# Joining the expert block and the final sum of a small language-model tower, with the last two groups' results kept on chip

## What is computed

```
merged = einsum('bked,bke->bed', tok, vals)          # 32 sequences x 32 experts x 256
h1 = gelu(einsum('bei,eih->beh', [merged, 1], w1))    # w1: 32 experts, 257 x 1024
o  = einsum('bej,ejo->beo', [h1, 1], w2)              # w2: 32 experts, 1025 x 256
out = zeros_like(x).at[b, idx].add(o * vals)          # each expert's row back to its 8 tokens
h = h + out
```

## Time and profile before

| what | value |
|---|---|
| median of 3 runs | 860.26 us (857.64 to 861.04) |
| the profiled execution's own time | 861.66 us |
| its span, first to last instruction | 859.9 us |
| mean TensorE clock granted | 0.937 |
| PE, DVE, POOL, ACT busy | 82%, 70%, 52%, 41% of the span |
| DMA of the experts' weights | 32 transfers of 2 MB |

### The profile page before, as it was taken

How to read it: one execution, slowest core, us unless ns; L and a number is a source line. 1 busy time by engine, 2 the same in 40 slices (tenths; PEclk the granted TensorE clock), 3 DMA queues, 4 the chain that set the end, 5 groups by cost and what they waited for, 6 DMA issues and landing times. The chain is left out here.

```text
span 859.9 us, 20461 instructions
## 1 busy us (share of the span) xinstructions
PE 701.9 (82%) x7740; PEld 479.6 (56%) x7740; DVE 600.9 (70%) x853; ACT 353.4 (41%) x563; POOL 447.4 (52%) x250
## 2 busy tenths in 40 slices
PE   6577679868999999999999999994899859766674
PEld 4466444436777777777777777763677524322232
DVE  3688548888999999999999999992577621000014
ACT  3366534434544455544554454542555321210000
POOL 1788400004999999999999999992122100000000
PEclk9699979997999999999999999996999969988895
DMA  4100000000001010000000000002920199999977
GB/s 113 50 2 0 0 0 0 0 0 16 14 11 37 14 37 12 10 8 12 12 12 10 9 12 12 15 15 66 401 87 2 30 367 409 413 414 421 413 313 251
DMA packets 47291, 86.34 MB, mean 100 GB/s; under 512 B 5552, under 2 KB 30704, under 8 KB 47120
## 3 DMA queue, kind: packets, MB, share of 16 engines
q1 hardware_dynamic: 43696, 83.33, 26.2%
q10 hardware_dynamic: 3552, 2.43, 0.9%
HBM read 76.31 MB, written 9.44 MB: 100 GB/s over the span
## 5 line engine op out<-in xcount | busy, mean ns | idle before, releaser
L907 POOL TENSOR_TENSOR read<-state,q_pos 128x1024 f32<-128x1024 f32 x128 | 300.3, 2365 | 28.5 <-DVE state L1016 22.4
L1016 DVE TENSOR_TENSOR_SCAN state<-fac,ps_up 128x1024 f32<-128x1024 f32 x128 | 289.9, 2277 | 8.6 <-ACT fac L951 8.6
L951 ACT ACTIVATE fac<-ps_xf 128x1016 f32<-128x1016 f32 x128 | 130.2, 1017 | 176.4 <-PE ps_xf L1050 162.8
L1050 PEld LDWEIGHTS ps_xf<-hot,xtab 64*128 64x128 f32 x2048 | 126.3, 189 | 58.0 <-ACT fac L951 43.4
L1050 PE MATMUL ps_xf<-hot,xtab 64*128 64x128 f32 x2048 | 149.2, 285 | 11.0 <-ACT fac L951 8.9
L1050 PE MATMUL ps_up<-hot,utab 64*128 64x128 f32 x2048 | 140.7, 277 | 18.3 <-DVE state L1016 18.3
L1050 PEld LDWEIGHTS ps_up<-hot,utab 64*128 64x128 f32 x2048 | 127.0, 190 | 23.8 <-issue 17.7
L916 POOL TENSOR_TENSOR utab<-tab 128x1024 f32 (+1 forms) x32 | 64.7, 2022 | 95.5 <-SPq L85 95.5
L1095 PE MATMUL ps_o<-read,sel 128*32 128x256 f32 x1024 | 82.7, 395 | 3.7 <-POOL read L907 3.7
L1669 DVE COPY h_t<-ps_ht 128x512 f32<-128x512 f32 x16 | 10.3, 686 | 86.1 <-PE ps_ht L1700 86.0
L1684 PE MATMUL ps<-w_sb,mq 128*32 128x512 f32 x256 | 38.4, 739 | 27.7 <-DMA w_sb<-in_L_ffn_w 22.6
(11 more groups left out here) (200 smaller groups left out, 953.4 us busy)
## 6 DMA issues: line engine op xcount, KB each, us to landing
w_sb<-in_L_ffn_w SPq DMA_DIRECT2D x32, 2048.0 KB, 19.2
rec_out<-osb SPq DMA_DIRECT2D x128, 32.0 KB, 1.5
ao<-rec_out SPq DMA_DIRECT2D x8, 512.0 KB, 4.1
out_dram<-h SPq DMA_DIRECT2D x8, 256.0 KB, 2.5
out_dram<-h ACTq DMA_DIRECT2D x8, 256.0 KB, 3.1
tok<-in_x SPq DMA_DIRECT2D x2, 512.0 KB, 8.1
exp_out<-eo SPq DMA_DIRECT2D x8, 128.0 KB, 18.6
oq<-exp_out SPq DMA_DIRECT2D x8, 128.0 KB, 3.0
```

Of the source, the lines that this page charges most:

```text
L907: nc.gpsimd.tensor_tensor(read[n % 2][:], state[n % 4][:].rearrange("p (b i t) -> p b i t", b=2, i=IB), q_pos[x.s][:, :, x.k].unsqueeze(2) ...
L951: nc.scalar.activation(fac[n % 2][:].rearrange("p (n t) -> p n t", t=T)[:, :, 1:], ps_x[:].rearrange("p (n t) -> p n t", t=T)[:, :, 1:], A ...
L1016: nc.vector.tensor_tensor_scan(state[n % 4][:], fac[n % 2][:], ps_u[n % 2][:], 0.0, ALU.mult, ALU.add)\
L1050: last = nc.tensor.matmul(dst[:, b * 512 + col * T:b * 512 + (col + 1) * T], stationary[rows], pos[rows], start=True, stop=True)
```

## The change

`experts` and `combine` become one block with its loops written out.

- PE reads `merged` directly; `mq` and its copies go. ACT loads the Gelu table before the first group.
- Only the results of groups 0 to 5 (24 experts, `STORED`) are stored. When ACT has seen the stores of both `eo` buffers land, ACT (no longer SP) reloads them into `oq` with four transfers of 24 rows by 8 KB.
- Group 6: DVE builds a 0/1 matrix `spread` in the place of `merged`, and PE permutes `eo[:, 0]` with eight matmuls (`spread_rows`) into the four PSUM banks that held `ps_1`. DVE adds that to `oq`, once the reload has landed.
- Group 7: `rows_of_last` permutes `eo[:, 1]` by rows with four matmuls, DVE copies them to `last_rows`, and a second set of four matmuls per quad (`output_last`) adds them, with `last_picks`. `last_picks` is made by 32 matmuls (`picks_of_last`) between the first layers of groups 0 and 1.
- The final sum's matmuls, additions and stores follow in the same block, each quad with eight matmuls in place of four.

The core of the diff, with the programs of ACT, SP, DVE and PE in this order:

```diff
+STORED = X - 2 * QB
...
-            def operands(i, s):
-                q = 2 * i + s
-                act.wait_ge(l2[s], START + 2 * i)
-                nc.scalar.copy(mq[s][:], merged[:, :, bass.ds(QB * q, QB)]).then_inc(mq_ok, 1)
...
+        sel_ok, h1_mm, gl, ht, htok, eo_ok = (sem(n) for n in ("sel_ok", "h1_mm", "gl", "ht", "htok", "eo_ok"))
...
+            for g in range(GROUPS):
+                hidden(g)
+                if g + 2 < GROUPS:
+                    selections(g + 2)
+            for s in range(2):
+                act.wait_ge(eo_st[s], START + 16 * (GROUPS // 2 - 1))
+            src = exp_out.rearrange("x (q j) e -> j x q e", j=QB)
+            for j in range(QB):
+                act.dma_start(oq[j * X:j * X + STORED], src[j, 0:STORED]).then_inc(f_ld, 16)
+            store_rows(act, 1)
...
-            for s in range(2):
-                store(TURNS - 1, s)
-            for s in range(2):
-                sp.wait_ge(eo_st[s], START + 16 * TURNS)
-            for h in range(2):
-                reload(h)
+            first_weights(2)
+            for g in range(2, GROUPS):
+                if g + 1 < GROUPS:
+                    first_weights(g + 1)
+                second_weights(g)
+                store(g - 2)
+            store_rows(sp, 0)
...
+            for g in range(GROUPS):
+                for h in range(2):
+                    hidden(g, h)
+                if g == GROUPS - 1:
+                    dve.wait_ge(row_mm, SPREAD_MM)
+                    dve.wait_ge(f_ld, START + 16 * QB)
+                    nc.vector.tensor_tensor(oq[:], oq[:], ps_s, ALU.add).then_inc(row_ok, 1)
+                results(g)
+                if g == GROUPS - 2:
+                    dve.wait_ge(h1_mm, START + GROUPS)
+                    nc.vector.tensor_tensor(spread, at_row[:].unsqueeze(2).broadcast_to([P, B, X]),
+                                            at_expert[:].unsqueeze(1).broadcast_to([P, B, X]), ALU.mult)\
+                        .then_inc(row_ok, 1)
+            dve.wait_ge(row_mm, ROWS_MM)
+            nc.vector.tensor_copy(last_rows[:], ps_p).then_inc(row_ok, 1)
+            for q in range(QUADS):
+                dve.wait_ge(f_mm, START + q + 1)
+                rows = h2[:, QB * q:QB * (q + 1)]
+                nc.vector.tensor_tensor(rows, ps_q[q % 2][:, :, 0:E], rows, ALU.add).then_inc(f_add, 1)
...
+            def first_layer(g):
+                s = g % 2
+                pe.wait_ge(gl, START + g - 1)
...
+            def picks_of_last():
+                pe.wait_ge(row_ok, STRIP)
+                for q in range(QUADS):
+                    at = QUADS - 1 - q
+                    for j in range(QB):
+                        rows = slice(j * X, (j + 1) * X)
+                        last = nc.tensor.matmul(ps_t[rows, q], strip[rows, at:at + X], picked[rows, q],
+                                                start=True, stop=True)
+                last.then_inc(row_mm, 1)
+            def spread_rows():
+                pe.wait_ge(row_ok, SPREAD)
+                pe.wait_ge(gl, START + GROUPS)
+                for q in range(QUADS):
+                    last = nc.tensor.matmul(ps_s[:, q], spread[:, QB * q:QB * (q + 1)].rearrange("p j x -> p (j x)"),
+                                            eo[:, 0], start=True, stop=True)
+                last.then_inc(row_mm, 1)
+            def rows_of_last():
+                pe.wait_ge(eo_ok, START + GROUPS)
+                for j in range(QB):
+                    last = nc.tensor.matmul(ps_p[j * X:(j + 1) * X],
+                                            ident[:].rearrange("p (n j) -> p j n", j=QB)[:, j],
+                                            eo[:, 1], start=True, stop=True)
+                last.then_inc(row_mm, 1)
+            def output_stored(q):
+                if q > 1:
+                    pe.wait_ge(f_add, START + q - 1)
+                for j in range(QB):
+                    rows = slice(j * X, (j + 1) * X)
+                    nc.tensor.matmul(ps_q[q % 2][:, j, 0:E], picked[rows, q], oq[rows, q], start=True, stop=False)
+            def output_last(q):
+                for j in range(QB):
+                    rows = slice(j * X, (j + 1) * X)
+                    last = nc.tensor.matmul(ps_q[q % 2][:, j, 0:E], last_picks[rows, q], last_rows[rows],
+                                            start=False, stop=True)
+                last.then_inc(f_mm, 1)
...
+            first_layer(0)
+            picks_of_last()
+            first_layer(1)
...
+            transpose_hidden(GROUPS - 1)
+            second_bias(GROUPS - 1)
+            spread_rows()
+            second_layer(GROUPS - 1, 0)
+            pe.wait_ge(row_ok, SUMS)
+            output_stored(0)
+            second_layer(GROUPS - 1, 1)
+            rows_of_last()
+            pe.wait_ge(row_ok, ROWS)
+            output_last(0)
+            for q in range(1, QUADS):
+                output_stored(q)
+                output_last(q)
```

More of the change, by code:

```diff
@@ L1567, in load_w2, with experts @@
         .then_inc(done[h], 16)
-def experts(nc, a, m, sem, sb):
-    ident, merged, exp_out, oq = m["ident"], m["merged"], m["exp_out"], m["oq"]
+def experts(nc, a, m, sem, sb, out):
+    ident, merged, exp_out, h2, picked = m["ident"], m["merged"], m["exp_out"], m["h2"], m["picked"]
     w1, w2, b1, b2, w1_ld, w2_ld = m["w1_sb"], m["w2_sb"], m["b1_sb"], m["b2_sb"], m["w1_ld"], m["w2_ld"]
-    mq = [sb(f"mq{s}", [P, KT, QB, B]) for s in range(2)]
     sel = [sb(f"sel{s}", [X, QB, B]) for s in range(2)]
@@ L1578, in experts @@
     eo = sb("eo", [P, 2, E])
[L1580 to L1589 removed]
+    oq = sb("oq", [P, QUADS, E])
@@ L1607, in _, with selections @@
-            operands(0, 0)
-            operands(0, 1)
-            with nc.scalar.Fori(0, TURNS - 1) as i:
-                for s in range(2):
-                    hidden(i, s)
-                    operands(i + 1, s)
-            for s in range(2):
-                hidden(TURNS - 1, s)
+            def selections(g):
+                if g > 1:
+                    act.wait_ge(l2[g % 2], START + 2 * (g // 2))
+                nc.scalar.copy(sel[g % 2][:], ident[0:X, QB * g:QB * (g + 1)].unsqueeze(2)
+                               .broadcast_to([X, QB, B])).then_inc(sel_ok, 1)
@@ L1618, in _ @@
             m["start"](sp)
[L1620 to L1632, removed]
@@ L1640, in second_weights @@
+            def second_weights(g):
                 for h in range(2):
[L1641 to L1651, removed]
@@ L1661, in _ @@
+            store_rows(sp, 0)
         @block.vector
         def _(dve):
[L1663 to L1669, removed]
-                    dve.wait_ge(l2[s], START + 2 * i + 2)
-                    dve.wait_ge(eo_st[s], START + 16 * i)
-                    nc.vector.tensor_copy(eo[:, s], ps_2[s][:, 0:E]).then_inc(eo_ok, 1)
+            ch = m["vch"]
@@ L1683, in first_layer @@
                         for j in range(QB):
-                            last = nc.tensor.matmul(ps_1[s][j * B:(j + 1) * B, cols], mq[s][:, k, j],
+                            last = nc.tensor.matmul(ps_1[s][j * B:(j + 1) * B, cols], merged[:, k, QB * g + j],
                                                     w1[s][:, j, k, cols], start=k == 0, stop=False,
@@ L1765, in _ @@
+            def output_stored(q):
+                if q > 1:
+                    pe.wait_ge(f_add, START + q - 1)
                 for j in range(QB):
                     rows = slice(j * X, (j + 1) * X)
-                    last = nc.tensor.matmul(ps[q % 2][:, j, 0:E], picked[rows, q], oq[rows, q], start=True, stop=True)
-                last.then_inc(f_mm, 1)
-        @block.vector
-        def _(dve):
-            for q in range(QUADS):
-                dve.wait_ge(f_mm, START + q + 1)
-                rows = h2[:, QB * q:QB * (q + 1)]
-                nc.vector.tensor_tensor(rows, ps[q % 2][:, :, 0:E], rows, ALU.add).then_inc(f_add, 1)
+                    nc.tensor.matmul(ps_q[q % 2][:, j, 0:E], picked[rows, q], oq[rows, q], start=True, stop=False)
@@ new lines, in _ @@
+            for g in range(GROUPS - 1):
+                transpose_hidden(g)
+                second_bias(g)
+                for h in range(2):
+                    second_layer(g, h)
+                if g + 2 < GROUPS:
+                    first_layer(g + 2)
+            transpose_hidden(GROUPS - 1)
[5 more added lines that the diff above has]
+            second_layer(GROUPS - 1, 1)
```

146 lines of the change are left out of this document (75 added, 71 removed).

## The result

The changed kernel takes 869.0 us (median of 4 runs, 866.9 to 869.8) against 859.85: ratio 1.0102, 95% interval 1.0079 to 1.0126. By the ratio it is 8.8 us slower (6.8 to 10.8). The forecast was 862.4, its range ended at 866.8.

What follows compares the result with a forecast made beforehand. The weight stream (712 to 834), then a serial end, was taken as the bound. Reload, sums, half layer and copies put the first addition at 848.0, not 845.9; with the old 14.0 tail, median 860.26 plus 2.1 gave 862.4, range 860.4 to 866.8.

Steps and rivals of the forecast that it cites:

- 2.1 us were predicted: Whole kernel: first addition of the final sum at 848.0 instead of 845.9, tail unchanged, so 2.1 us slower.
- 0.8 predicted: Head of the experts block: without the mq copies and their wait, the whole weight stream moves forward by 0.8 us.
- the picks and the spread product are hidden: Experts block: picks (2.6 us on PE) run under queued loads; spread product and spread_rows (5.2 us) under the reload wait.
- 5.2: Reload after group 5's store lands: 2.0 us fixed plus 0.79 MB at 246 GB/s, 5.2 us; bounds 4.0 and 6.4.
- fewer engines: Rival on the reload: 24 rows use 12 of 16 engines, 185 GB/s, 6.3 us, result +3.2 (863.5); chance 0.15.
- the rise 3.4 us after work began: Last half layer: PE starts at 1.2 GHz about 841.6, full clock at about 845.0, layer ends at 845.5.
- 0.8 and 3.1 stood: Before the final sum: output_stored(0) takes 0.8 us to 842.4, then the last half layer runs to 845.5.
- the clock comes late: Rival: half layer and next matmuls at 1.2 GHz, first addition +3.4, slow early tail, result +4.7 (865.0); chance 0.24.
- the old 14.0: Tail from first addition to end: at full clock 1.25 to 1.3 us a quad, so 14.0 us as before.
- PE's waiting for code: Tail: an example of something outside the listed cases, making the kernel slower; no size given, chance 0.03.
- I add 2.1 to the median: Base: the 2.1 us is added to the median 860.26, 1.4 under the profiled execution's 861.66, giving 862.4.
- its two terms: Lower end of the range, given as 860.4: reload at its lower bound and a tail at 1.25 us a quad.

Runs made afterwards that it cites:

- c4: The kernel before, unchanged, third of three more profiles, last half layer at 2.4 GHz; 155.9 us from the last merged copy to the end.
- e9: Against the changed kernel: groups 0 to 6 permuted on chip by matmuls, no store or reload through DRAM; 852.8 us, ratio 0.9916 to the kernel before.
- c2: The kernel before, unchanged, first of three more profiles, with the clock's fall near 600 us; the three took 857.8, 857.8 and 859.8 us.
- e8: Changed kernel with stores on ACT's queue, reload of 32 rows in 8 KB pieces, PE's half layer before the sums; 861.5 us, 1.0027 to before.
- e12: e8 with one reload transfer into 128 partitions in place of four into 32, rows in wrong order; 857.2 us, ratio 0.9983 to the kernel before.
- e1: Changed kernel with PE's last half layer and rows_of_last, and DVE's two copies, ahead of the sums; 862.9 us, ratio 1.0046 to the kernel before.
- e5: Changed kernel with stores on ACT's queue and the last half layer and DVE's two copies ahead of the sums; 866.3 us, 1.0082 to before.

## Why the prediction was wrong

The direction and the mechanism held, the size did not: 2.1 us were predicted, 8.3 found against c4. The steps that failed are three terms of the sum (the reload, the rise of the clock, the tail) and its base. What held: the store of group 5 lands behind the weights; the reload begins there, not in the stream; PE idles through it; the half layer stands behind the sums; the stream is 0.9 to 1.3 us earlier, with 0.8 predicted (last weights at 131.1 and 130.7 us after the last merged copy, 132.0 in before and c4); the picks and the spread product are hidden; the tail's matmuls run at full clock. Four terms were off.

- **The reload, "5.2".** From the store's landing to DVE's start it was 7.4. The four issues took 3.8 us where 0.47 each was carried over from ACT's output stores: with pieces of 1 KB a transfer took 0.77 to issue, the first 1.38 (with 8 KB pieces 1.7 for all four). And the rate was 184 GB/s in place of 246, on 12 engines. The rival "fewer engines" was the right mechanism at a chance of 0.15; its price of 1.1 us left out the issues. Together +2.1.
- **The clock in the half layer, "the rise 3.4 us after work began".** It came at about 850, some 6 us after PE's start at 844.06, and so only behind the half layer. The first quad's sums took 1.24 and the half layer 3.62, where 0.8 and 3.1 stood: +0.9. (0.8 leaves out the end of the last record; the earlier trace rows had 1.27 for eight records at this clock.) That is about what "the clock comes late" said for its first part; its second, a slow tail, did not come. That the tail ran at full clock was forecast, but for a rise that was to come 5 us earlier. With hand-overs the way from the store's landing to the first addition was 17.3 us and not 14.2.
- **The tail, "the old 14.0".** 15.4, although the additions ran at 1.25 us a quad. That pace is not the reason: e9 has it too, and 14.0. What ends the tail is a late output store. A 16 KB piece of code is fetched at 858 to 860 among the stores; in before and in e9 the last fetch comes at 845.8 and 839.0, ahead of the first store (847.15 and 839.98). Two answers on transfers, after (858 to 860) and e9 (838 to 840):

```profile
q8 instruction: 1, 0.02, 3.6%
...
out_dram<-h SPq DMA_DIRECT2D x2, 256.0 KB, 4.0
```

```profile
q8 instruction: 1, 0.02, 3.3%
...
out_dram<-h SPq DMA_DIRECT2D x1, 256.0 KB, 2.2
```

In all five profiles of before and in e9 every fetch lies ahead of the first output store, and the tail is 14.0. In all fourteen others one falls 2 to 6 us behind the first store, and the tail is 15.4 to 16.2. The prediction spoke of more code and counted nothing for it, with the weight stream in mind; in the tail it gave PE's waiting for code 0.03. That the fetch is the cause was argued from this and not tried by itself.

- **The base, "I add 2.1 to the median".** The profiled execution was 1.4 us over the median, and I took that as scatter elsewhere. It lay in the very layer that the sum starts from: 3.57 where c2 to c4 have 1.93, so the change was compared with a half layer at the low clock. +1.7.

The forecast of 2.1, 3.1 from the store's landing to the first addition, 1.4 of tail and 1.7 of base make 8.3, as found. The range had a slip of its own: by its two terms its lower end is 862.4 - 1.2 - 0.4 = 860.8, not 860.4; nothing hangs on it.

The gain that the change could have had also has its answer. With the reload as it is written, taking the last two groups off the way through DRAM gains nothing while the others stay on it. In SP's queue the store is late (the change). On ACT's it is early, but the reload slows the stream: e8's last weights land 6.8 us behind e9's, of which 3.7 remain in e12 with the wide reload and 3.1 go with the narrow one. e12's first addition is 3 us ahead of before's, so a wide reload in the right order might gain; that stays open. e9 takes the way out altogether: its first addition is 13.7 us ahead of the change's and 6.9 ahead of before's (141.9).

## What to carry to other kernels

- Before work is put "under" a stream that fills the DMA engines, look at what it does to the stream: bytes over rate is the least it costs. Here four transfers into 32 partitions each ran at about 240 GB/s and dragged a stream of some 420 GB/s down to that; one into 128 did not.
- A wait for a late transfer belongs behind all work that does not need it. Here one wait ahead of a half layer, whose weights were there, cost 5.4 us (e1).
- Look at two or three executions before taking the profiled one as the base: a layer in the changed stretch at another clock was 1.7 of 8.3 us. And where TensorE has idle time under a stream, a permutation by matmul can replace a round trip through DRAM altogether (e9).

## What was not expected of the hardware

- Three of five executions of the same program ran its last half layer in 1.98 us, two in 3.54 to 3.63, with the clock at 1.00 and 0.50. In these five the two kinds go with whether the clock fell back once more near 600 us, 230 us earlier: where it did, the layer at the end ran at full clock. Why is open, and in e5, where PE idled 5.7 us ahead of the layer, it fell and the layer still took 3.64.
- A transfer of 24 rows in 1 KB pieces takes 0.77 us to issue on ACT's queue (median of four), one of 32 rows 0.65, with 8 KB pieces 0.31 to 0.56.
- A total rate of 231 to 246 GB/s at a DMA share of 0.96 to 1.02: the share says that the engines are occupied, not that they move data at their rate. The weights' own packets ran at some 245 GB/s for their share beside the narrow reload (e8), at some 400 beside the wide one (e12).
